# Mamba block on one Trainium2 core: the dt projection's halves on two row groups, the output projection as 64-column products on two column groups

## The reference

```python
seq = pixel_shuffle(layernorm_over_channels(x), 2)      # 2304 positions of 128 channels, after one token
u, z = split(seq @ in_proj_w.T)                         # 256 channels each
u = silu(causal_conv4(u) + conv_b)
dt, B, C = split(u @ x_proj_w.T, [8, 24])               # 8, 16 and 16 rows
dt = softplus(dt @ dt_proj_w.T + dt_proj_b)             # 256 channels
h = exp(dt * A) * h + (dt * u) * B                      # 16 states per channel, along the sequence
y = (sum over states of h * C + u * D) * silu(z)
out = y @ out_proj_w.T                                  # 128 channels
x = x + pixel_unshuffle(out)
```

## Time and profile before

| what | value |
|---|---|
| median of 3 runs | 1304.27 us (1303.02 to 1305.35) |
| the profiled execution's own time | 1302.34 us |
| its span | 1300.6 us |
| busy in the span | PE 1100.8 us (85%), PEld 660.8 us (51%), DVE 1157.0 us (89%), ACT 806.6 us (62%), POOL 1110.7 us (85%) |
| chain that ended last, shares | POOL 29%, PE 22%, DVE 21%, issue 21%, ACT 6% |
| dt projection L863 | 96 records (24 units, 2 products, 2 records each), 37.9 us busy |
| output projection L730 | 96 records, 34.9 us busy |
| copy into XDT, L525 | 24, 11.7 us busy |

### The profile page before, as it was taken

The page is one execution under the profiler, slowest core; times in us unless marked ns, Lnnn a source line. Parts: engine busy times, 40 slices in busy tenths (PEclk is TensorE's granted clock), DMA queues, the critical chain, the costliest instruction groups (busy, mean ns, idle before and its releaser), DMA issues.

```text
span 1300.6 us, 13356 instructions
## 1 busy us (share of the span) xinstructions
PE 1100.8 (85%) x3818; PEld 660.8 (51%) x3818; DVE 1157.0 (89%) x1345; ACT 806.6 (62%) x1496; POOL 1110.7 (85%) x747
## 2 busy tenths in 40 slices
PE   6588888888888988988988988988988888887997
PEld 4344554544544544544544544545545545444887
DVE  1399999999999999999999999999999999999751
ACT  2476765766766666766666666666757657656230
POOL 4299899898898898898898898898998998988750
PEclk8789999999999898898998998999998998998998
DMA  6221321222221221221222212213212213215351
GB/s 160 75 96 53 104 97 58 87 94 77 80 98 68 92 99 57 99 99 61 98 82 78 99 64 96 99 57 104 99 56 104 99 56 116 96 63 168 115 159 30
DMA packets 64539, 116.80 MB, mean 90 GB/s; under 512 B 34218, under 2 KB 47954, under 8 KB 64466
## 3 DMA queue, kind: packets, MB, share of 16 engines
q1 hardware_dynamic: 64466, 115.96, 26.3%
HBM read 108.47 MB, written 7.47 MB: 89 GB/s over the span
## 4 chain that ended last, share of the span: by engine, by line
POOL 29%; PE 22%; DVE 21%; issue 21%; ACT 6%; POOLq 0%; SPq 0%; DVEq 0%; DMA 0%; ACTq 0%
POOL SCAN L413 16%; DVE SCAN L967 13%; PE Yp L693 8%; POOL SCAN L425 6%; DVE SCAN L922 4%; PE PP L772 3%; PE PP L839 3%; PE PP L722 2%; PE PP L819 2%; POOL XN L450 1%; PE PP L812 1%; POOL GATES L418 1%; DVE GATES L951 1%; ACT SGZ L598 1%; POOL XN L441 1%
## 5 line engine op out<-in xcount | busy, mean ns | idle before, releaser
L967 DVE TENSOR_TENSOR_SCAN SCAN<-DA,CAR,SCAN 128x384 f32<-128x384 f32 x768 | 729.8, 1000 | 38.4 <-POOL SCAN L425 36.5
L413 POOL TENSOR_TENSOR SCAN<-SCAN,CS 128x768 f32<-128x768 f32 x384 | 693.9, 1821 | 27.2 <-DVE SCAN L967 26.8
L490 ACT ACTIVATE DA<-UDT,A 128x384 f32<-128x384 f32 x768 | 441.8, 581 | 389.6 <-DVE SCAN L967 386.3
L693 PE MATMUL Yp<-SCAN,IDENT 128*128 128x384 f32 x1536 | 593.7, 512 | 97.5 <-POOL SCAN L413 89.6
L693 PEld LDWEIGHTS Yp<-SCAN,IDENT 128*128 128x128 f32 x1536 | 289.7, 198 | 304.9 <-POOL SCAN L413 143.5
L922 DVE TENSOR_TENSOR SCAN<-UDT,BB 128x768 f32<-128x768 f32 x288 | 268.7, 933 | 11.1 <-PE BB L675 9.2
L425 POOL TENSOR_TENSOR SCAN<-UDT,BS 128x768 f32<-128x768 f32 x96 | 175.4, 1827 | 0.0
L839 PE MATMUL PP<-XN,WT 128*128 128x384 f32 x384 | 139.8, 499 | 0.0
L839 PEld LDWEIGHTS PP<-XN,WT 128*128 128x128 f32 x384 | 75.8, 199 | 56.6 <-issue 11.8
L445 POOL TENSOR_TENSOR UDT<-UDT 128x768 f32<-128x768 f32 x24 | 43.5, 1811 | 69.9 <-DVE UDT L1056 69.9
L675 PE MATMUL BB<-PT,SEL 96*128 96x384 bf16 x288 | 98.3, 342 | 4.6 <-DVE SCAN L922 4.6
(11 more groups left out here) (161 smaller groups left out, 1155.4 us busy)
## 6 DMA issues: line engine op xcount, KB each, us to landing
CS<-bc_rows SPq DMA_DIRECT2D x96, 768.0 KB, 4.0
BS<-bc_rows SPq DMA_DIRECT2D x24, 768.0 KB, 6.0
out<-XN SPq DMA_DIRECT2D x32, 192.0 KB, 2.4
X<-in_x SPq DMA_DIRECT2D x24, 192.0 KB, 3.6
X<-in_L_ffn_memory_tokens SPq DMA_DIRECT2D x16, 256.0 KB, 3.0
XN<-in_L_ffn_memory_tokens SPq DMA_DIRECT2D x16, 256.0 KB, 3.1
bc_rows<-XDT SPq DMA_DIRECT2D x24, 48.0 KB, 1.5
X<-in_L_ffn_memory_router SPq DMA_DIRECT2D x1, 512.0 KB, 3.8
```

Of the source, the lines that this page charges most:

```text
L413: pool.tensor_tensor(M[:, n1 % MRING], HB[:, n1 % HRING], over_halves(CS[:, n1 % CRING]), ALU.mult).then_inc(m_ready, 1)
L490: act.activation(DA[:, h, 0:T], DT[:, par, h], ACT.Exp, scale=A[:, h, n:n + 1])\
L693: last = pe.matmul(Yp[:, h, 0:T], IDENT[:, :], M[:, n3 % MRING, h], start=n3 == 0, stop=n3 == NS - 1)
L967: dve.tensor_tensor_scan(HB[:, s % HRING, h], DA[:, h, 0:T], HB[:, s % HRING, h], CAR[:, ds(J * NS * HALVES + s * HALVES + h, 1)], ALU.mul ...
```

## The change

- The dt projection of half 0 moves to partitions 32 to 56: tile position (32, 0), 25 rows. Half 1 stays at partition 96. For this XPT's part 1 has B in its columns 32 to 47 as before, dt in 48 to 55 and what was C's last half in 56 to 63; DTW has a second copy of half 0's weights in rows 32 to 56, whose rows 32 to 47 are zero; and row 56 of XDT stays one, as row 104 does.
- Per unit ACT gets one more copy, rows 32 to 55 of PP into XDT, ahead of L525.
- The output projection becomes four products of 64 columns: for each half, columns 0 to 63 into PSUM partitions 0 to 63 (tile position (0, 0)) and columns 64 to 127 into partitions 64 to 127 (tile position (0, 64)).
- At the start there are two more DMAs on SP's queue and five more small copies on ACT. The token's own dt projection (L715) is unchanged.

```diff
 GROUPS = NS // GRP
 XROW0 = 64
+DTROW0 = 48
+XROWS0 = DTROW0 + RANK
...
-        N_WLOADS = 8
+        N_WLOADS = 10
...
             sp.dma_start(DTNAT[:, :, DTROW:XROWS],
                          dt_w.rearrange("(k e) r -> e k r", e=P)).then_inc(w_loaded, 16)
+            sp.dma_start(DTNAT[:, 0, DTROW0:XROWS0], dt_w[0:P]).then_inc(w_loaded, 16)
+            sp.dma_start(DTNAT[:, 0, XROWS0:XROWS0 + 1],
+                         dt_b[0:P].rearrange("(e r) -> e r", r=1), allow_slow_non_contiguous=True).then_inc(w_loaded, 16)
...
                     for part in range(PARTS):
-                        act.activation(XPT[:, h, part * BC:(part + 1) * BC], xp[:, RANK:RANK + BC], ACT.Copy)
+                        cols = NS if part == 1 else BC
+                        act.activation(XPT[:, h, part * BC:part * BC + cols], xp[:, RANK:RANK + cols], ACT.Copy)
+                    act.activation(XPT[:, h, XROWS0:2 * BC], xp[:, XROWS0 - BC + RANK:BC + RANK], ACT.Copy)
+                    act.activation(XPT[:, h, DTROW0:XROWS0], xp[:, 0:RANK], ACT.Copy)
                     act.activation(XPT[:, h, DTROW:XROWS], xp[:, 0:RANK], ACT.Copy)
+                act.activation(DTW[BC:XROWS0 + 1, 0], PP[BC:XROWS0 + 1, 1, 128:256], ACT.Copy)
+                for h in range(HALVES):
                     last = act.activation(DTW[DTROW:XROWS + 1, h], PP[DTROW:XROWS + 1, 1, 128 + h * P:256 + h * P],
                                           ACT.Copy)
...
                     positive(act, rows_written, 16 * f)
+                    act.activation(XDT[BC:XROWS0, :], PP[BC:XROWS0, 1, 0:T], ACT.Copy)
                     act.activation(XDT[XROW0:XROWS, :], PP[XROW0:XROWS, 1, 0:T], ACT.Copy).then_inc(hi_ready, 1)
...
                     for h in range(HALVES):
-                        last = pe.matmul(PP[:, 0, 0:T], OPT[:, h], VV[:, h], start=h == 0, stop=h == 1)
+                        for c in (0, P // 2):
+                            last = pe.matmul(PP[c:c + P // 2, 0, 0:T], OPT[:, h, c:c + P // 2], VV[:, h],
+                                             start=h == 0, stop=h == 1, tile_position=(0, c))
                     last.then_inc(op_ready, 1)
...
-                        last = pe.matmul(PP[:, h, 0:T], DTW[DTROW:XROWS + 1, h], XDT[DTROW:XROWS + 1, :],
-                                         start=True, stop=True, tile_position=(DTROW, 0))
+                        row, end = ((BC, XROWS0 + 1), (DTROW, XROWS + 1))[h]
+                        last = pe.matmul(PP[:, h, 0:T], DTW[row:end, h], XDT[row:end, :],
+                                         start=True, stop=True, tile_position=(row, 0))
                     last.then_inc(dtp_ready, 1)
```

## The result

The changed kernel takes 1304.86 us (median of 20 runs, 1303.05 to 1307.08) against 1302.91 of the kernel before (20 runs): ratio 1.0013, 95% interval 1.0007 to 1.0019, that is +1.7 us (0.9 to 2.5; the two medians are 1.95 apart, which lies inside). The forecast was +2.2 us, about the same time as before; its 1306.4 us lies 1.5 above the measured median, and 1.4 of that is its starting point, the median of three runs (1304.27) where twenty give 1302.91. The size is right, partly by luck: several terms of the sum were off, in both directions. The profiled execution took 1306.79 us (span 1305.0), at the upper edge of its runs, so its extra 4.4 us of span must not be read as the change's price.

The account below looks back on a forecast made before the run. POOL and DVE alternately bound the middle, PE the end; the start is nearly serial. Small copies 0.63 + first front 0.49 + unit 0 0.37 - dt 0.52 + end 1.20 = 2.2 us, giving 1306.4 us, range 1303.3 to 1314.

Parts of the forecast that it names:

- The middle doesn't move: Middle units: shifts of PE and the added copy on ACT vanish in existing waits; the unit stays 49.67 us.
- the rival "a gain": Middle: earlier dt projection lets ACT's softplus chain start earlier, up to 0.65 us a unit, 14 us, 1290; chance 0.03.
- one record of four, only neighbours can meet: dt projection on PE: program order lets one record overlap, 0.32 us less, 0.52 in the first front.
- The prediction's own signs: PE slots expected in the changed profile: about 1.16 us for the dt projection, about 1.9 for the output projection.
- Entering and leaving a tiled form: Output projection on PE: switching tiling mode costs 0.28 us, taken from the dt projection's row.
- the 0.32 for a missing overlap: Output projection on PE: only neighbours meet, so eight records fill five slots, 0.32 us more.
- The copies: Added copy on ACT: 0.49 us in the first front, 0.37 in unit 0, nothing in the middle.
- The five small copies: Start, on ACT: four into XPT at 0.09 us each and one into DTW at 0.27, 0.63 on the chain.
- The two added DMAs: Start, SP's queue: they delay dt's bias, but ACT's first user has 3.5 us of cover, so 0.
- The rival "no overlap": Tiled f32 products on PE don't overlap: sum 11 us, 1315, or 1308.9 without the middle's push; chance 0.24.
- Its push in the middle: At L805 PE shifts 1.00 us against 0.51 of room; DVE starts 0.5 late in 13 units, 6.4 us.
- The rival "everything is cheaper": PE's projections: halves and column groups run wholly side by side; sum 1.0 us, 1305.3; chance 0.13.

Follow-up runs that it names:

- the one with three projections: The kernel before with the output projection done three times over; ratio 1.0173 (1.0158 to 1.0189).
- the order experiment: The changed kernel with the output projection's four products ordered by column group, both halves for columns 0 to 63 first; ratio 1.0006 (0.9996 to 1.0015).
- the kernel before again: The kernel before, unchanged, executed once more for its profile; 1303.85 us in one execution.

## Why the prediction was right, and where it was not

**The middle doesn't move**: right, and for the reasons given. The unit is 49.67 to 49.71 us in every version but the one with three projections (so the rival "a gain" is out as well), and a PE that is 0.5 us ahead (dt) or a busier ACT (copy) both end in longer or renamed waits.

**The overlap**: the step "one record of four, only neighbours can meet" failed. The prediction's own signs were 1.16 and 1.9 us for the two slots; measured are 0.85 and 1.45. The Trainium skill ("TensorE: Matmul & The Clock Gate", Part 3) has tiles overlap as a whole, and these slots agree with it. Its further sentence, that matmuls start and end in the program's order, is not borne out here for the starts: with four records of one column group ahead of four of the other the eight still pair up. In the first front the dt projection saves, by the leg after the second rounding product, 0.4 to 0.8 us where PE's clock was high at its beginning (2.62 and 2.20 against 3.00; the moment at which it fell differs among them too) and 1.3 where it was low (3.03 against 4.30); I had 0.52. The number is near, the mechanism isn't: that half 0 runs beside the token's dt projection, which brings its start forward by 0.45 us (0.86 at the low clock), was not in the prediction.

**Entering and leaving a tiled form**: taken as 0.28 from the dt projection's row, in front of it and in it together. In the middle the column groups cost 0.24: 0.09 in front (1.38 against 1.29) and 0.15 in the slot. That is nearly the forecast. At the end they cost more. Timelines of PE, kernel before and, second, after:

```profile
1274.91 7.50 PE L772 MATMUL DA<-GATES,XN 128*128 128x128 f32 x32
1282.25 1.46 PE L730 MATMUL PP<-VV,OPT 128*128 128x384 f32 x4
1283.54 7.50 PE L772 MATMUL DA<-GATES,XN 128*128 128x128 f32 x32
1290.88 1.03 PE L737 MATMUL PP<-X,MEANW 128*128 128x96 f32 x8
```
```profile
1279.51 7.50 PE L785 MATMUL DA<-GATES,XN 128*128 128x128 f32 x32
1286.94 1.51 PE L742 MATMUL PP<-VV,OPT 128*64 128x384 f32 x8
1288.38 7.73 PE L785 MATMUL DA<-GATES,XN 128*128 128x128 f32 x32
1295.95 1.03 PE L750 MATMUL PP<-X,MEANW 128*128 128x96 f32 x8
```

From start to start that is 7.34, 1.29 and 7.34 before and 7.43, 1.44 and 7.57 after: 0.09 in front, 0.15 in the projection and 0.23 behind it. The last part is in the weight loads. PE's weight loads (PEld), before and, second, after:

```profile
1283.22 0.31 PEld L772 LDWEIGHTS DA<-GATES,XN 128*128 128x128 f32 x1
```
```profile
1288.38 0.31 PEld L785 LDWEIGHTS DA<-GATES,XN 128*128 128x128 f32 x1 [0.60 <-issue]
```

Before, the first load of the 32 products' weights starts 0.32 us ahead of the first product, under the projection's last record. After, it starts only with the product. In this stream each record starts 0.23 us after the one before and each weight load takes 0.33, so a late load is not made up, while in the middle, where a load takes 0.19 and a record 0.32, it is. The first of the two output projections of the end is alike (6.18 us before from the sum in front of it to the next sum, 6.66 after). So 0.47 each and 0.94 in all, against 1.20 forecast: the 0.32 for a missing overlap is really 0, and the 0.28 for the switch is really 0.47.

**The copies**: in the first front 0.49 as forecast (1.62 against 1.13). In unit 0 0.37 forecast; where PE's clock was low at the x projection, DVE waits 0.57 for the exp of scan 5 instead of 0.07, so 0.5; where it was high (the order experiment; the kernel before again) there is no such wait, and it cost nothing. The five small copies 0.30 instead of 0.63. In ACT's timeline the next instruction starts 0.06 us after each of the four copies of 8 columns, not 0.09; the change also put the copies into DTW behind all those into XPT, where they had stood between the halves. That the rest of the difference is this reordering was not tested. The two added DMAs, priced at 0, don't show: ACT's first small copy starts between 14.0 and 15.4 us with them and between 14.1 and 15.1 without.

**The sum** by these: 0.30 + 0.49 + (0 to 0.5) + 0.94 less 0.4 to 1.3 = 0.4 to 1.8, measured 1.7 (0.9 to 2.5). In the forecast of 2.2 two terms were too high (small copies by 0.3, end by 0.3), the gain of the dt projection was too small where the clock was low, and unit 0 was off in either direction with the clock. That the total came out within half a microsecond is in part such errors being small and in part luck. (The range's low end was miscounted too: 1304.27 less the scatter of 1.25 is 1303.0, not 1303.3. The result doesn't hang on it.)

**The rival "no overlap"** is excluded by the slots. Its push in the middle was also wrongly priced: it took idle time before a matmul as the room of PE, but a record's duration holds 0.16 us through the array, and the next could have started earlier. Start to start, PE has 0.42 free at 620.84 and 0.52 at 628.54, with DVE's 0.5 together 1.4 instead of 1.07. Twice the projection (1.29) indeed cost nothing there. **The rival "everything is cheaper"** named the right overlap; its sum of 1.0 lacked 0.2 us at each projection of the end (0.47 instead of 0.28) and had the small copies too dear.

## What to carry to other kernels

Products on different row or column groups ran side by side as a whole, even in f32 with two records each, and for the column groups in both orders that were tried, so two small products on two row groups took two slots of 0.32 us and the switch, where they had taken four. Splitting a product that fills the array into column groups gave nothing and cost the switch (0.24 us), and more (0.47) where short products that wait on their weights stand behind it. A small product can also run beside an unrelated one of another row group that stands ahead of it, as the token's did here. And a faster slot pays only where its engine is late: test that by doing the work twice, which shows the room of every later deadline at once, and measure PE's room from start to start, not by the idle time in front of a matmul.

## What the runs showed of the hardware that was not expected

- A later product on a free group overtakes an earlier one on a busy group (the 0.58 us record L877 at 43.76 between the records of L726, and the order experiment's 1.45 us).
- Entering and leaving column groups cost 0.09 us in front of the product and 0.15 in its slot, and 0.23 more behind it where short full-array products follow, whose first weight load no longer ran ahead.
- PE's clock in the first 60 us differs between executions of one program: the first leg with the dt projection took 3.00 and 4.30 us in two profiles of the kernel before, the latter with the clock at its lower level from the first rounding product on.
